# A decoder's quantised linear layer and long convolution, each as one streamed turn over eight batches

## The chip, the core and the metric

One core of a Trainium2 chip runs the whole program. The metric is the device time of one execution in microseconds (us); what is given for a kernel is the median of its runs.

## What is computed

The reference is a decoder of twelve sublayers over x of 8 batches x 256 rows x 256 columns, each followed by x = layernorm(x + sublayer(x)). The sixth and the seventh are at issue; the fifth, an attention with a side input over 16 heads, stands ahead of them.

```python
def quant_fp8(x):                                   # sixth: quantised linear layer
    amax = jnp.max(jnp.abs(x)).astype(jnp.float32)  # over the whole tensor
    scale = jnp.minimum(FP8_MAX / jnp.maximum(amax, 1e-12), FP8_MAX)   # FP8_MAX = 448
    return jnp.clip(x * scale, -FP8_MAX, FP8_MAX).astype(jnp.float8_e4m3fn), 1.0 / scale
w_fp8, w_scale = quant_fp8(weight)
x_fp8, x_scale = quant_fp8(x2d)
acc = jnp.matmul(x_fp8.astype(jnp.float32), w_fp8.astype(jnp.float32).T)
out2d = (acc * (x_scale * w_scale) + bias).astype(jnp.bfloat16)

p = (jnp.einsum('bld,de->ble', x, proj_w) + proj_b).reshape(B, L, order + 1, D)   # seventh: order = 2
v = p[:, :, 0, :]
for stage in range(order):
    vf = jnp.fft.rfft(v, n=fft_size, axis=1)
    ff = jnp.fft.rfft(filter_time[stage], n=fft_size, axis=1)
    v = jnp.fft.irfft(vf * ff, n=fft_size, axis=1)[:, :L, :] * p[:, :, stage + 1, :]
```

## The kernel before

Five engines run their own instruction lists: PE (matmuls and transposes into eight PSUM banks), DVE, ACT, POOL and SP (which issues the DMAs). Their only ties are semaphores. A `turn` (L215) is one block with a list for each engine, closed by a barrier of all engines. The order on each engine is the order in which the code issues. x stays in SBUF twice: `x_tok` with rows on partitions (16 tiles of 128x256) and `x_feat`, turned, with columns on partitions. All weights share one array, `weights`; `follow_weights` (L230) waits for a stage's weights and starts the load of the next stage's. Temporaries lie in `work`, and the profile calls them by that name.

The **side attention** (L2054) is one turn that streams 32 units (batch and four heads) through all engines; a step of its loop issues parts of several units, and `batch_statistics`, `batch_power`, `batch_normalise`, `batch_turn` and `batch_store` (L614 to L655) do the layernorm of one batch: statistics on DVE, the power -1/2 on POOL, the normalisation on DVE, four transposes on PE, the copy into `x_feat` on ACT.

The **quantised linear layer** (L2271) has a first turn: DVE takes the maximum of |x_tok| and of |w| on each partition (L2288, L2290), POOL takes them over the partitions (L2305), DVE works out the scales and rounds w to the values of e4m3 (L2259). A device loop then goes over four groups of two batches, a turn each: DVE rounds 1024 columns of x_feat in six operations (L2263 to L2268), PE multiplies (8 calls on bf16), DVE scales, adds bias and x (L2334, L2337), and the layernorm follows; its last copies are L420.

The **long convolution** (L2357) replaces the FFT by matmuls with 512x256 matrices `dft` and `idft`. A turn loads the weights, a turn makes the spectra of the two filters, then `run_late` (L364) issues the body for group 0, for groups 1 to 3 in a device loop, and a last turn with the tail alone. A body copies x (L272), projects it to three gates (24 calls of `mm`, L249; DVE adds the bias, L2442), and twice goes: four banks of forward transform (8 calls of 512 columns), eight products by the filter on DVE (L2453), four additions or subtractions on POOL (L2427), eight inverse calls (L2411), gate on DVE (L2459). The layernorm of the group before, the "late tail", stands between projection and transform. An fp32 matmul call shows as two MATMUL records in the profile.

## Time and profile before

| what | value |
|---|---|
| median of three runs | 2859.42 us (2854.62 to 2860.02) |
| the profiled execution, its own time | 2862.32 us |
| its span, first to last instruction | 2860.6 us |
| PE busy | 2333.3 us (82%), 12834 instructions |
| DVE busy | 1433.5 us (50%) |
| ACT busy | 1025.7 us (36%) |
| POOL busy | 672.5 us (24%) |
| mean granted clock of PE | 0.90 of 2.4 GHz |

The shares are means over twelve stages with different limits, so they don't say what binds one of them. A timeline row gives start, length, engine, line, operation, output and inputs, and in brackets how long the engine had idled and what released it. A granted clock of 1.00 is 2.4 GHz, 0.50 is 1.2 GHz; a stretch between the two had some of each.

### The profile page before, as it was taken

Reading aid. Unit: us, or ns where it says so; the run is one execution under the profiler, and the core shown is the slowest. Engines: PE = TensorE matmul, PEld = TensorE weight load, DVE = VectorE, ACT = ScalarE, POOL = GpSimd, SP = SyncE. Lnnn points to the kernel's source line nnn. Section 1 sums busy time; section 2 is a strip of 40 time slices with the busy share of each in tenths; the row PEclk is TensorE's granted clock in tenths of the full one; section 3 lists DMA queues with packets and bytes.
Section 4 is the critical chain, followed back from the end, with each engine's and each line's share of the span. In section 5 each row is a group of like instructions: output and inputs, shape, how many; then the busy total and the mean of one; then the engine's idle time right before and its main releaser. Section 6 shows DMA issues by size and latency. Waiting matters only on the chain. (4 is left out here: it accounts for less than half of the span.)

```text
span 2860.6 us, 38992 instructions
## 1 busy us (share of the span) xinstructions
PE 2333.3 (82%) x12834; PEld 1622.3 (57%) x12834; DVE 1433.5 (50%) x4235; ACT 1025.7 (36%) x2587; POOL 672.5 (24%) x609
## 2 busy tenths in 40 slices
PE   7983599878789438878667879879799899899898
PEld 5762477655467324447246656546356577466576
DVE  3554122447668554345412266645577543577454
ACT  3432111155446200006212226534366543466432
POOL 1113311200034102210443310065343200434111
PEclk9996799979789669988688989989899999999899
DMA  9041211290000100002157721130000000000000
GB/s 236 2 191 48 74 46 35 70 132 1 1 7 1 39 17 0 0 8 115 47 160 208 199 74 27 30 139 1 30 1 2 1 1 0 1 1 1 19 23 19
DMA packets 121167, 143.58 MB, mean 50 GB/s; under 512 B 47507, under 2 KB 101013, under 8 KB 119184
## 3 DMA queue, kind: packets, MB, share of 16 engines
q1 hardware_dynamic: 112240, 120.16, 15.7%
q0 software_dynamic: 8736, 20.99, 2.0%
q8 instruction: 105, 1.72, 0.3%
q14 instruction: 86, 0.70, 0.1%
HBM read 96.18 MB, written 47.90 MB: 50 GB/s over the span
## 5 line engine op out<-in xcount | busy, mean ns | idle before, releaser
L249 PE MATMUL bank<-work,weights 128*128 128x256 f32 (+4 forms) x2048 | 491.4, 397 | 65.0 <-DMA work<-in_weights 29.4
L249 PE MATMUL bank<-weights,work 128*128 128x256 f32 (+4 forms) x1680 | 450.8, 409 | 26.5 <-ACT work L272 16.9
L249 PEld LDWEIGHTS bank<-work,weights 128*128 128x128 f32 (+1 forms) x2048 | 345.7, 195 | 182.0 <-issue 50.7
L249 PEld LDWEIGHTS bank<-weights,work 128*128 128x128 f32 (+1 forms) x1680 | 314.5, 199 | 130.3 <-issue 59.0
L633 POOL TENSOR_TENSOR work<-work,minus_half 128x2 f32<-128x2 f32 x80 | 57.7, 722 | 801.2 <-DVE work L626 801.2
L249 PE MATMUL bank<-weights,x_feat 128*128 128x512 f32 (+2 forms) x384 | 166.2, 557 | 24.2 <-PEq L211 13.2
L249 PE MATMUL bank<-x_feat,weights 128*128 128x256 f32 (+3 forms) x400 | 119.3, 473 | 35.7 <-PEq L211 31.0
L249 PE MATMUL bank<-work 128*128 128x120 f32 (+4 forms) x358 | 82.2, 373 | 78.9 <-DVE work L2268 47.3
L3958 ACT ACTIVATE work<-work 128x128 f32<-128x128 f32 (+1 forms) x256 | 137.5, 545 | 1.7 <-DVE work L4030 1.6
L1523 DVE TENSOR_TENSOR work<-bank,work 128x384 f32<-128x384 f32 (+1 forms) x64 | 31.4, 491 | 190.0 <-ACT work L1441 190.0
L249 PEld LDWEIGHTS bank<-x_feat,weights 128*128 128x128 f32 (+1 forms) x400 | 79.6, 217 | 64.9 <-issue 51.5
L249 PEld LDWEIGHTS bank<-work 128*128 128x128 f32 (+2 forms) x358 | 59.6, 197 | 95.9 <-DVE work L2268 48.9
L249 PEld LDWEIGHTS bank<-weights,x_feat 128*128 128x128 f32 x384 | 68.7, 197 | 77.5 <-issue 59.1
L2898 ACT ACTIVATE work<-bank,work 128x128 f32<-128x128 f32 x124 | 38.9, 365 | 152.7 <-PE bank L249 144.0
L4350 DVE SCALAR_TENSOR_TENSOR work<-bank,weights,work 128x256 f32<-128x256 f32 x96 | 45.6, 482 | 86.6 <-ACT work L4288 85.5
L2756 POOL DMA_INDIRECT rows_back<-work x62 | 60.4, 974 | 115.4 <-DVE work L2994 97.0
L2994 DVE TENSOR_SCALAR work<-bank,work 128x256 f32<-128x256 f32 x62 | 30.0, 484 | 114.6 <-PE bank L249 98.6
L658 ACT COPY x_feat<-bank 128x512 f32<-128x512 f32 x64 | 37.4, 585 | 139.3 <-PE bank L650 138.9
L3773 POOL TENSOR_TENSOR work<-work,minus_half 128x8 f32<-128x8 f32 x32 | 52.4, 1638 | 142.3 <-DVE work L4074 142.3
L1341 POOL DMA_INDIRECT rows_back<-work x40 | 39.0, 974 | 195.4 <-DVE work L1531 195.4
L4288 ACT ACTIVATE work<-bank,weights 128x256 f32<-128x256 f32 x80 | 38.1, 476 | 127.9 <-PE bank L249 127.7
L4022 DVE CUSTOM_DVE_ANT_0 work<-bank,work 128x128 f32<-128x128 f32 (+1 forms) x256 | 75.9, 352 | 14.7 <-PE bank L3821 14.7
(462 smaller groups left out, 4750.2 us busy)
## 6 DMA issues: line engine op xcount, KB each, us to landing
weights<-in_weights SPq DMA_DIRECT2D x62, 256.0 KB
weights<-in_weights SPq DMA_DIRECT2D x1, 12296.0 KB, 35.5
weights<-in_weights SPq DMA_DIRECT2D x1, 9360.0 KB, 25.1
weights<-in_weights SPq DMA_DIRECT2D x1, 8488.0 KB, 23.9
work<-rows_in SPq DMA_DIRECT2D x62, 129.0 KB
rows_in<-ident SPq DMA_DIRECT2D x2, 3968.0 KB, 40.1
weights<-rows_back SPq DMA_DIRECT2D x8, 768.0 KB, 5.3
work<-rows_in SPq DMA_DIRECT2D x8, 645.0 KB, 4.2
```

Source lines behind the costliest of these rows:

```text
L249: ins = nc.tensor.matmul(out, lhsT, rhs, start=(i == 0), stop=(i == len(pairs) - 1))
L633: nc.gpsimd.tensor_tensor(t.rstd[:, n, :], t.rstd[:, n, :], K.minus_half[:, 0:2], ALU.pow).then_inc(K.S.rstd_done, 1)
L658: copy(K.x_feat[:, :, b * L:(b + 1) * L], K.bank[bank][:, :].rearrange("p (k t) -> p k t", k=KT)).then_inc(K.S.xT_stored, 1)
L1341: nc.gpsimd.indirect_dma_start(K.rows_back, bass.IndirectOffsetOnAxis(ap=to, axis=0), y[:, r, :], None, bounds_check=TOP * T - 1, oob_is_e ...
L1523: nc.vector.tensor_tensor(hT[:, q % 2, m, 0:n], K.bank[2 * (at % 2) + 1][:, 0:n], gelu[:, at % 2, 0:n], ALU.mult).then_inc(S.inner_stored, 1)
L2756: nc.gpsimd.indirect_dma_start(K.rows_back, bass.IndirectOffsetOnAxis(ap=to, axis=0), y[:, r, :], None, bounds_check=TOP * T - 1, oob_is_e ...
L2898: ins = nc.scalar.activation(hT[:, j % 2, m, :], K.bank[2 + j % 2][:, m * P:(m + 1) * P], ACT.Relu, bias=bias1[:, j % SETS, m:m + 1])
L3773: nc.gpsimd.tensor_tensor(rk, norm[:, 1, :], K.minus_half[:, 0:H], ALU.pow).then_inc(S.rk_done, 1)
L3958: ins = nc.scalar.activation(probs[:, u % 3, s, at:at + width], probs[:, u % 3, s, at:at + width], ACT.Exp, bias=bias[:, u % 2, i, s:s + 1 ...
L4022: ins = nc.vector.tensor_tensor_reduce(probs[:, u % 3, s, at:at + width], K.bank[SM[s]][:, at:at + width], seen[:, at:at + width], 1.0, -3 ...
L4288: nc.scalar.activation(gelu[:, n % 2, :], K.bank[n % RING][:, L:2 * L], ACT.Gelu, bias=W["b1"][:, layer, HT + f:HT + f + 1]).then_inc(S.ge ...
L4350: nc.vector.scalar_tensor_tensor(out=hid[rows, b % 2, f, :], in0=K.bank[n % RING][rows, 0:L], scalar=W["b1"][rows, layer, f:f + 1], in1=ge ...
```

## The change

Nothing changes in the arithmetic of a result but its grouping. Both stages become one turn each, unrolled over eight batches with double buffers, in the manner of the side attention.
- The maximum of |x_tok| is taken batch by batch inside the side attention, on DVE, one step after the batch is normalised, and that of |w| at its step 3. `quant_buffers` places the results and the rounded w behind the weights of the linear layer.
- In the linear layer, two transposes on PE with a reduction and a broadcast copy on DVE take the place of POOL's reduction over partitions. ACT multiplies x by its scale, DVE clamps it and makes the power of two (three operations of 512 columns), POOL adds and subtracts it.
- In the convolution a batch has its own 256-column calls: 12 of projection, 16 forward, 16 inverse, 4 transposes. The projection reads `x_feat` itself. The filter's spectra are stored with one part twice, so that two products of 512 columns replace four of 256; POOL's additions are 128x256. The load of the weights is waited for inside the turn, and that of the next stage's weights starts there.

Removed lines are in the functions printed above; the diff is cut to its core.

```diff
+def quant_buffers(K):
+    at = HIGH + words(5)
+    q = Names()
+    q.w16 = K.weights[:, at:at + KT * D // 2].bitcast(BF16).rearrange("p (k d) -> p k d", k=KT)
...
+    return q
 def side_attention(nc, K):
...
         @block.sync
...
+            def peak(b):
+                v.wait_ge(S.x_normed, b + 1)
+                nc.vector.tensor_reduce(q.peak[:, b:b + 1], K.x_tok[:, 2 * b:2 * b + 2, :].rearrange("p i d -> p (i d)"),
+                                        AX.X, ALU.max, apply_absolute_value=True)
...
                     c.finish(v, b)
+                if (b := at_step(t - BACK - 6, QUADS, B)) is not None:
...
                     store_v(b)
+                if t == 3:
+                    weights_are_in(v, K, 5)
+                    nc.vector.tensor_reduce(q.peaks[:, 1:2], next_w.rearrange("p k d -> p (k d)"), AX.X, ALU.max,
+                                            apply_absolute_value=True)
...
 def quantised_linear(nc, K):
...
+        def _(p):
+            def rounded(b):
+                p.wait_ge(S.k_rounded, b + 1)
+                nc.gpsimd.tensor_tensor(scaled[:, b % 2, :, :], scaled[:, b % 2, :, :], power[:, b % 2, :, :], ALU.add
+                                        ).then_inc(S.pool_step, 1)
+                p.wait_ge(S.pool_step, b + 1)
+                if b >= 2:
+                    p.wait_ge(S.y_done, b - 1)
+                nc.gpsimd.tensor_tensor(x16[:, b % 2, :, :], scaled[:, b % 2, :, :], power[:, b % 2, :, :], ALU.subtract
+                                        ).then_inc(S.xn_stored, 1)
...
+            def products(b):
+                pe.wait_ge(S.xn_stored, b + 1)
+                if b == 0:
...
+                if b >= 2:
+                    pe.wait_ge(S.bias_added, b - 1)
+                for i in range(2):
+                    ins = mm(nc, K.bank[b % 2][:, i * D:(i + 1) * D],
+                             [(x16[:, b % 2, k, i * P:(i + 1) * P], q.w16[:, k, :]) for k in range(KT)])
+                ins.then_inc(S.y_done, 1)
...
+            pe.wait_ge(S.max_done, 1)
+            nc.tensor.transpose(K.bank[4][0:2, 0:P], q.peaks, K.ident[:]).then_inc(S.aux_done, 1)
+            pe.wait_ge(S.spread_done, 1)
+            nc.tensor.transpose(K.bank[5][:, 0:2], spread_peaks[0:2, :], K.ident[0:2, 0:2]).then_inc(S.aux_done, 1)
...
+            def scale_x(b):
+                if b >= 2:
+                    a.wait_ge(S.xn_stored, b - 1)
+                nc.scalar.activation(scaled[:, b % 2, :, :], K.x_feat[:, :, b * L:(b + 1) * L], ACT.Copy, scale=q.scale[:, 0:1]
...
+            a.wait_ge(S.inverse_done, 1)
...
+            def magnitude(b):
+                v.wait_ge(S.xc_scaled, b + 1)
+                x = scaled[:, b % 2, :, :]
+                then(nc.vector.tensor_scalar(x, x, 448.0, -448.0, ALU.min, ALU.max))
+                then(nc.vector.tensor_scalar(power[:, b % 2, :, :].bitcast(I32), x.bitcast(I32), 0x7F800000, None,
+                                             ALU.bitwise_and))
+                nc.vector.tensor_scalar(power[:, b % 2, :, :], power[:, b % 2, :, :], 2.0 ** -6, 1.5 * 2.0 ** 20,
+                                        ALU.max, ALU.mult).then_inc(S.k_rounded, 1)
+            def residual(b):
+                x2 = K.x_tok[:, 2 * b:2 * b + 2, :]
+                v.wait_ge(S.y_done, b + 1)
+                nc.vector.scalar_tensor_tensor(
+                    out=y16[:, b % 2, :, :], in0=K.bank[b % 2][:, :].rearrange("p (i d) -> p i d", i=2),
+                    scalar=q.out_scale, in1=W["bias"].broadcast_to([P, 2, D]), op0=ALU.mult, op1=ALU.add
+                    ).then_inc(S.bias_added, 1)
+                v.wait_ge(S.bias_added, b + 1)
+                nc.vector.tensor_tensor(x2, x2, y16[:, b % 2, :, :], ALU.add).then_inc(S.residual_done, 1)
+                batch_statistics(nc, v, K, tail, b)
+            nc.vector.tensor_reduce(q.peaks[:, 0:1], q.peak, AX.X, ALU.max).then_inc(S.max_done, 1)
             v.wait_ge(S.aux_done, 1)
...
+            then(nc.vector.tensor_reduce(q.most[0:2, :], K.bank[4][0:2, 0:P], AX.X, ALU.max))
+            nc.vector.tensor_copy(spread_peaks[0:2, :], q.most[0:2, :].broadcast_to([2, P])).then_inc(S.spread_done, 1)
+            v.wait_ge(S.aux_done, 2)
+            then(nc.vector.tensor_scalar(q.scale, K.bank[5][:, 0:2], 1e-12, None, ALU.max))
+            then(nc.vector.reciprocal(q.scale, q.scale))
+            nc.vector.tensor_scalar(q.scale, q.scale, 448.0, 448.0, ALU.mult, ALU.min).then_inc(S.inverse_done, 1)
+            v.wait_ge(S.inverse_done, 1)
+            then(nc.vector.reciprocal(q.back, q.scale))
+            then(nc.vector.tensor_tensor(q.out_scale, q.back[:, 0:1], q.back[:, 1:2], ALU.mult))
+            for t in range(STEPS):
+                if (b := at_step(t, 1, B)) is not None:
+                    magnitude(b)
+                if t == 0:
+                    round_to_e4m3(nc, then, q.w16, W["w"], q.scale[:, 1:2], w_scaled, w_power).then_inc(S.root_done, 1)
+                if (b := at_step(t - 1, 1, B)) is not None:
+                    residual(b)
+                if (b := at_step(t - 2, 1, B)) is not None:
+                    batch_normalise(nc, v, K, tail, b)
...
 def long_convolution(nc, K):
...
+    ORDER, STEPS = 2, B + 4
+    GATES, HALVES, BACK, X = (0, 1, 2), (3, 4), (5, 6), 7
+    gates = A(2, ORDER + 1, 2 * D)
+    filt = A(ORDER, 2, 3 * D)
+    part = A(2, 2, 2 * D)
+    spec = A(2, 4, D)
...
+            def combine(q):
+                for f in range(2):
+                    p.wait_ge(S.probs_done, 2 * q + f + 1)
+                    if q >= 2:
+                        p.wait_ge(S.out_done, q - 1)
+                    for which, op in ((0, ALU.subtract), (1, ALU.add)):
+                        ins = nc.gpsimd.tensor_tensor(spec[:, q % 2, f + 2 * which, :], part[:, f, which, 0:D],
+                                                      part[:, f, which, D:2 * D], op)
+                    ins.then_inc(S.pool_step, 1)
...
+            def project(b, e):
+                if b:
+                    pe.wait_ge(S.q_stored, 3 * (b - 1) + e + 1)
+                for i in range(2):
+                    ins = mm(nc, K.bank[GATES[e]][:, i * D:(i + 1) * D],
+                             [(K.x_feat[:, k, b * L + i * P:b * L + (i + 1) * P], W["proj"][:, k, e * D:(e + 1) * D])
+                              for k in range(KT)])
+                ins.then_inc(S.qk_done, 1)
...
+            def forward(b, s):
+                q = 2 * b + s
+                if s:
+                    pe.wait_ge(S.gate_done, b + 1)
+                else:
+                    pe.wait_ge(S.q_stored, 3 * b + 1)
+                for f in range(2):
+                    if q:
+                        pe.wait_ge(S.probs_done, 2 * (q - 1) + f + 1)
+                    else:
+                        pe.wait_ge(S.aux_stored, 1)
+                    for m in (f, f + 2):
+                        ins = mm(nc, K.bank[HALVES[f]][:, m // 2 * D:(m // 2 + 1) * D],
+                                 [(W["dft"][:, k, m * P:(m + 1) * P], gates[:, b % 2, 0, k * D:(k + 1) * D])
+                                  for k in range(2)])
+                    ins.then_inc(S.scores_done, 1)
+            def backward(b, s):
+                q = 2 * b + s
+                pe.wait_ge(S.pool_step, 2 * q + 2)
+                if b == 0:
+                    pe.wait_ge(S.aux_stored, 2)
+                else:
+                    pe.wait_ge((S.gate_done, S.y_added)[s], b)
+                for m in range(2):
+                    ins = mm(nc, K.bank[BACK[s]][:, m * D:(m + 1) * D],
+                             [(W["idft"][:, n, m * P:(m + 1) * P], spec[:, q % 2, n, :]) for n in range(4)])
+                ins.then_inc(S.out_done, 1)
...
+            for t in range(STEPS):
+                if (b := at_step(t, 1, B)) is not None:
+                    forward(b, 0)
+                if (b := at_step(t + 1, 1, B)) is not None and b:
+                    project(b, 0)
+                    project(b, 1)
+                if (b := at_step(t - 1, 1, B)) is not None:
+                    backward(b, 1)
+                if (b := at_step(t, 1, B)) is not None:
+                    backward(b, 0)
+                if (b := at_step(t + 1, 1, B)) is not None and b:
+                    project(b, 2)
+                if (b := at_step(t - 2, 1, B)) is not None:
+                    turn_x(b)
+                if (b := at_step(t, 1, B)) is not None:
+                    forward(b, 1)
...
+                a.wait_ge(S.aux_done, s + 1)
...
+                    nc.scalar.copy(filt[:, s, f, 0:2 * D], bank[:, :])
+                    ins = nc.scalar.copy(filt[:, s, f, 2 * D:3 * D], bank[:, 0:D])
+                ins.then_inc(S.aux_stored, 1)
...
+            def store_gates(b, e):
+                v.wait_ge(S.qk_done, 3 * b + e + 1)
+                if b >= 2:
+                    v.wait_ge((S.scores_done, S.gate_done, S.residual_done)[e], (4 * b - 4, b - 1, b - 1)[e])
+                nc.vector.tensor_tensor(gates[:, b % 2, e, :].rearrange("p (i d) -> p i d", i=2),
+                                        K.bank[GATES[e]][:, :].rearrange("p (i d) -> p i d", i=2),
+                                        W["bproj"][:, :, e * D:(e + 1) * D].broadcast_to([P, 2, D]), ALU.add
+                                        ).then_inc(S.q_stored, 1)
+            def filtered(b, s):
+                q = 2 * b + s
+                if q < 2:
+                    v.wait_ge(S.aux_stored, q + 1)
+                for f in range(2):
+                    v.wait_ge(S.scores_done, 2 * q + f + 1)
+                    if q:
+                        v.wait_ge(S.pool_step, 2 * (q - 1) + f + 1)
+                    for which in range(2):
+                        ins = nc.vector.tensor_tensor(part[:, f, which, :], K.bank[HALVES[f]][:, :],
+                                                      filt[:, s, f, which * D:(which + 2) * D], ALU.mult)
+                    ins.then_inc(S.probs_done, 1)
+            def gate(b):
+                v.wait_ge(S.out_done, 2 * b + 1)
+                v.wait_ge(S.q_stored, 3 * b + 2)
+                nc.vector.tensor_tensor(gates[:, b % 2, 0, :], K.bank[BACK[0]][:, :], gates[:, b % 2, 1, :], ALU.mult
+                                        ).then_inc(S.gate_done, 1)
+            def residual(b):
+                x2, y = K.x_tok[:, 2 * b:2 * b + 2, :], gates[:, b % 2, 2, :]
+                v.wait_ge(S.out_done, 2 * b + 2)
+                v.wait_ge(S.q_stored, 3 * b + 3)
+                nc.vector.tensor_tensor(y, K.bank[BACK[1]][:, :], y, ALU.mult).then_inc(S.y_added, 1)
...
+            for t in range(STEPS):
+                if (b := at_step(t, 1, B)) is not None:
+                    filtered(b, 0)
+                if (b := at_step(t + 1, 1, B)) is not None and b:
+                    store_gates(b, 0)
+                    store_gates(b, 1)
+                if (b := at_step(t - 1, 1, B)) is not None:
+                    residual(b)
+                if (b := at_step(t, 1, B)) is not None:
+                    gate(b)
+                if (b := at_step(t - 1, 1, B)) is not None:
+                    batch_normalise(nc, v, K, tail, b)
+                if (b := at_step(t + 1, 1, B)) is not None and b:
+                    store_gates(b, 2)
+                if (b := at_step(t, 1, B)) is not None:
+                    filtered(b, 1)
```

PE in the long convolution, before: a pass of the loop over groups, from the late tail's transposes to the end of the first of two filter stages (`bankN` is a PSUM bank, 128x512 the output of a call).

```order
L413 MATMUL bank6<-ident,work 128x128 x4
L413 MATMUL bank7<-ident,work 128x128 x4
L249 MATMUL bank0<-work,weights 128x512 x2
L249 MATMUL bank2<-work,weights 128x512 x2
L249 MATMUL bank1<-work,weights 128x512 x2
L249 MATMUL bank3<-work,weights 128x512 x2
L2411 MATMUL bank4<-work,weights 128x512 x2
L2411 MATMUL bank5<-work,weights 128x512 x2
```

The same engine now, one step of the stream: forward transform of batch b (banks 3, 4), projection of b+1 (0, 1, 2), inverse of b-1 (6) and of b (5), transposes of b-2 (7), second forward transform of b.

```order
L249 MATMUL bank3<-work,weights 128x256 x4
L249 MATMUL bank4<-work,weights 128x256 x4
L249 MATMUL bank0<-weights,x_feat 128x256 x4
L249 MATMUL bank1<-weights,x_feat 128x256 x4
L249 MATMUL bank6<-work,weights 128x256 x8
L249 MATMUL bank5<-work,weights 128x256 x8
L249 MATMUL bank2<-weights,x_feat 128x256 x4
L650 MATMUL bank7<-ident,x_tok 128x128 x4
L249 MATMUL bank3<-work,weights 128x256 x4
L249 MATMUL bank4<-work,weights 128x256 x4
```

Between a forward transform and its inverse there stood nothing of another batch before; now there stand the projection of the next batch and an inverse of the one before.

DVE in the linear layer now, one step: clamp and power of batch b, residual and statistics of b-1, normalisation of b-2.

```order
L2377 TENSOR_SCALAR work<-work 128x512
L2378 TENSOR_SCALAR work<-work 128x512
L2380 TENSOR_SCALAR work<-work 128x512
L2386 SCALAR_TENSOR_TENSOR work<-bank,weights 128x512
L2391 TENSOR_TENSOR x_tok<-x_tok,work 128x512
L619 BN_STATS work<-x_tok 128x6 x2
L623 BN_AGGR work<-work 128x2 x2
L626 TENSOR_SCALAR work<-work 128x2
L641 TENSOR_SCALAR x_tok<-x_tok,work 128x256 x2
```

Before, all of this was one chain per group of two batches, with the multiplication by the scale and both roundings on DVE too.

## Rows read from the trace of the kernel before

**Rows 1.** Busy time by stretch, with granted clock (PEclk)
```profile
core 0: us, PE busy (x) PEld busy (x) DVE busy (x) ACT busy (x) POOL busy (x), PEclk, DMA share, GB/s
826.00:945.00 119.00, 116.14 (x913) 82.66 (x911) 102.95 (x203) 72.67 (x126) 51.98 (x33) 1.00 0.01 1
...
983.00:1051.00 68.00, 16.02 (x64) 9.89 (x64) 49.16 (x100) 6.90 (x12) 5.98 (x8) 0.50 0.00 0
...
1065.40:1111.50 46.10, 39.13 (x112) 20.71 (x112) 18.58 (x29) 0.62 (x1) 9.99 (x8) 1.00 0.00 0
1111.50:1167.20 55.70, 44.43 (x120) 23.80 (x120) 22.23 (x44) 2.35 (x4) 11.47 (x10) 0.90 0.00 1
```

**Rows 2.** Timeline (start, length, what, idle before), PE, convolution
```profile
1054.18 8.71 PE L249 MATMUL bank<-weights 128*128 128x256 f32 x32 [3.99 <-PEq L211]
1066.13 10.63 PE L249 MATMUL bank<-weights,work 128*128 128x256 f32 x48 [3.24 <-ACT work L272]
1077.55 7.13 PE L249 MATMUL bank<-work,weights 128*128 128x512 f32 x16 [0.78 <-DVE work L2442]
...
1112.40 12.08 PE L249 MATMUL bank<-weights,work 128*128 128x256 f32 x48 [4.35 <-ACT work L272]
...
1129.84 10.10 PE L249 MATMUL bank<-work,weights 128*128 128x512 f32 x16 [4.49 <-DVE work L2442]
```

**Rows 3.** Timeline, DVE, end of side attention to end of convolution
```profile
961.33 0.69 DVE L747 TENSOR_TENSOR x_tok<-x_tok,bank 128x512 f32<-128x512 f32 x1 [6.61 <-PE bank L249]
...
963.12 0.17 DVE L626 TENSOR_SCALAR work<-work 128x2 f32<-128x2 f32 x1
964.10 0.73 DVE L641 TENSOR_SCALAR x_tok<-x_tok,work 128x256 f32<-128x256 f32 x2 [0.81 <-POOL work L633]
967.98 4.42 DVE L2288 TENSOR_REDUCE work<-x_tok 128x1 f32<-128x4096 f32 x1 [3.14 <-PEq L211]
972.31 0.68 DVE L2290 TENSOR_REDUCE work<-weights 128x1 f32<-128x512 f32 x1
977.07 0.17 DVE L2295 TENSOR_SCALAR work<-work 128x2 f32<-128x2 f32 x1 [4.09 <-POOL work L2305]
...
978.47 0.43 DVE L2264 TENSOR_SCALAR work<-work 128x512 f32<-128x512 f32 x1
...
980.58 0.69 DVE L2268 TENSOR_TENSOR work<-work 128x512 bf16<-128x512 f32 x1
...
989.75 0.75 DVE L2334 SCALAR_TENSOR_TENSOR work<-bank,work,weights 128x512 bf16<-128x512 f32 x1 [1.13 <-PE bank L249]
990.66 0.69 DVE L2337 TENSOR_TENSOR work<-work,x_tok 128x512 f32<-128x512 bf16 x1 [0.16 <-DVE work L2334]
...
1050.34 0.69 DVE L420 COPY x_feat<-bank 128x512 f32 x1 [1.32 <-PE bank L413]
...
1282.83 0.69 DVE L420 COPY x_feat<-bank 128x512 f32<-128x512 f32 x1 [1.21 <-PE bank L413]
```

**Rows 4.** Timeline, PE and ACT: half clock, stage ends
```profile
965.80 0.59 ACT L658 COPY x_feat<-bank 128x512 f32<-128x512 f32 x1 [8.34 <-PE bank L650]
...
988.68 1.89 PE L249 MATMUL bank<-work 128*128 128x256 bf16 x8 [22.92 <-DVE work L2268]
995.85 2.12 PE L413 MATMUL bank<-ident,work 128*128 128x128 f32 x8 [5.28 <-DVE work L327]
...
1284.82 1.94 PE L2505 MATMUL bank<-ident,weights 128*128 128x128 f32 x8 [2.03 <-PEq L211]
```

**Rows 5.** Timeline, side attention: DVE beside POOL, and DVE's wait
```profile
886.58 1.79 POOL L2077 TENSOR_TENSOR work<-work 128x960 f32<-128x960 f32 x1 [1.64 <-DVE work L2237]
...
886.85 1.99 DVE L641 TENSOR_SCALAR x_tok<-x_tok,work 128x256 f32<-128x256 f32 x2
...
896.75 1.22 DVE L2230 TENSOR_TENSOR work<-bank,weights 128x480 f32<-128x480 f32 x2 [2.07 <-PE bank L2118]
```

**Rows 6.** Timeline, long convolution: DVE and POOL side by side
```profile
1081.28 2.49 DVE L2453 TENSOR_TENSOR work<-bank,work 128x512 f32<-128x512 f32 x4 [3.79 <-PE bank L249]
...
1082.65 2.50 POOL L2427 TENSOR_TENSOR work<-work 128x512 f32<-128x512 f32 x2 [34.41 <-DVE work L2453]
```

222 lines of the change are left out of this document (77 added, 145 removed).

## The prediction

> **What bounds the kernel now.** The program is a row of stages with a barrier between them, so I read stage by stage. First the table of stretches [rows 1]. The side attention fills PE: 116.14 of 119 us at clock 1.00. The quantised linear layer fills nothing: PE works 16.02 of 68.00 us, DVE 49.16. Of the long convolution's four group bodies the first takes 46.10 us with PE busy 39.13, the second 55.70 with PE 44.43 and DVE 22.23; the other two are like it. Then the timelines of one group. PE's work at full clock is a projection (10.63 us), four blocks of 7.13 us and, from the second group on, eight transposes [rows 2]. Between them PE waits for DVE and POOL, and in the later groups it starts at half clock: the projection takes 12.08, the first transform 10.10. So the convolution is a chain of waits around about 40 us of PE work per group, and its bound should be PE. The linear layer is a chain on DVE [rows 3]: one reduction of all x_tok (4.42 us), 4.09 us idle for POOL's reduction over partitions, then four groups in 68 us, with DVE idle at each hand-over (1.13 us ahead of L2334).
>
> **Linear layer.** Before, it runs from DVE's first instruction at 967.98 to the end of the last copy, 1050.34 + 0.69 = 1051.03: 83.05 us [rows 3]. After, I build it up in the order of its DVE rows.
> - Start. A reduction of 128x8, a transpose, a reduction of 2x128, a copy, a transpose and three small operations take the place of 9.1 us (967.98 to 977.07). Small DVE operations are 0.17 long and about 0.20 apart, six of them 1.2; two transposes at half clock, 0.27 each by 2.12 / 8 [rows 4], with hand-overs of about 0.2 each, 1.0. ACT scales from 970.2. Its 0.6 and the three operations of the clamp and the power (0.43 each, 0.46 apart, 1.35 together) end at 972.3. The Trainium skill (GPSIMD Engine Reference, Engine selection) wants a reduction over partitions on GpSimd; the 4.09 us of idle speak for PE in this case, and by that rule the start would keep about 3 us more.
> - Rounding of w, on DVE beside POOL's rounding of batch 0: four operations at 0.46 and two at 0.72, 3.3 us, plus about 2.5 if two POOL operations of 1.27 hold it up. Ends at 978.1.
> - A steady step on DVE: clamp and power 1.35, scalar_tensor_tensor to the end of the residual 1.60 (989.75 to 991.35), statistics 1.25 (the end of the residual at 962.02 to 963.29), normalise 0.73, 0.12 of waits: 5.05 us. POOL's load is 2 x 1.27 + 0.70 = 3.2, PE's 1.89 / 2 + 1.06 = 2.0, ACT's 1.2. DVE sets the pace. POOL's result for batch b comes some 4.5 us after the clamp of b ends and is read 5 us after it, so this wait is just covered.
> - Contention. In the side attention a normalise of 2 x 256 columns takes 1.99 us where POOL has just begun a 1.79 us operation, against 0.73 without one [rows 5]: it stood still for 1.26. Here POOL runs two large operations per batch beside DVE. Bounds: 0 and 2 x 1.26 per step; I take 0.65, since much of what DVE does then reads PSUM, as L2453 does, which runs at its 0.62 a piece beside POOL [rows 6]. The Trainium skill (SBUF — State Buffer, section SBUF: two separate sides) calls this an exclusive lock of a port pair, taken by DVE's two-port modes and also by DVE operations with two SBUF inputs; with that the residual's add would be held up too, about 0.7 a step, so 5.75 instead of the 5.05 without contention. The row of 1.99 agrees for the normalise; no row here shows the case of two SBUF inputs.
> - So 978.1, first clamp and residual 4.9, six steps of 5.7, then residual 7 and normalise 6 (4.1), and power wait, normalise 7, transposes at half clock and store (2.5): 1023.8. The layer takes 55.8 us: **27.2 us less**. Bounds 22 and 34 (steps of 6.4 and 5.05).
>
> **Long convolution.** Before: 1051.03 to 1283.52 (1282.83 + 0.69 [rows 3]), 232.5 us. After, with PE never waiting in the steady steps:
> - PE's work does not change. The 512-column calls become twice as many of 256 columns, and 16 MATMUL records of 512 cost 7.13 us, 48 of 256 cost 10.63 [rows 2]: 0.446 and 0.221 each, the same per column. Eight transposes take 1.06, half of their 2.12 at half clock [rows 4]. Per two batches 10.63 + 4 x 7.13 + 1.06 = 40.2; four times, 160.8. The filters' 32 records at 0.221 are 7.1.
> - Cold clock once. The filters cost 8.71 instead of 7.1, the second group 4.4 us more than the first [rows 2]. Bounds 1.6 and 4.4, I take 3.0. Each of three later groups pays 4.4 now, and this goes.
> - The start, 1.3 (1283.52 to 1284.82, where the next stage's PE begins [rows 4]). The load's own turn, the filters' turn and the last tail's turn go, with their barriers: the weights are issued a layer earlier in both kernels and are there.
> - Waits at the end. The last forward transform must pass DVE (two of 0.62 after 0.16) and POOL (two of 128x256) before the inverse. POOL's 128x256 is in no row; 128x512 is 1.27 [rows 6], so 0.64 to 1.27 each: 2.8 to 4.0, I take 3.2. The gate of batch 7 has a transpose less and no projection behind it: 0.4.
> - Tail after the last product: 5.06 as in the side attention (961.33 to 966.39 [rows 3, 4]) plus 0.16 and 0.86 for the multiplication ahead of it, less 0.5 of transposes already counted: 5.6.
> Sum 160.8 + 7.1 + 3.0 + 1.3 + 3.2 + 0.4 + 5.6 = 181.4: **51.1 us less**.
>
> Does PE really not wait? Take the order of the step. The first inverse of batch b comes 7.1 us after its spectrum (8 calls of projection, 8 of inverse, 0.44 a call). DVE and POOL need 0.16 + 1.3 + 0.07 + 1.3 to 2.5: under 4.1. A half of the transform is 1.77 us, DVE takes it away in 1.5, and the bank is wanted again 1.77 after its end: slack 0.25, the thinnest place. The gate needs 0.9 behind the inverse, the projection and the transposes cover 2.3; DVE must have finished the residual of b-1 by then (2.9 of 3.5). DVE's load per batch is 3 x 0.62 + 8 x 0.62 + 0.7 + 2.9 + 0.7 = 11.2 of 20.1 us, POOL's 8 x 0.64 to 1.27 plus 0.7: 5.8 to 10.9.
>
> **Side attention.** Eight reductions of 128x512 (0.68 each, as L2290 [rows 3]) and one of w. That of w stands where DVE idles at the stage's start. DVE idles 2.07 us behind the place of the others in each batch, and PE has no wait there [rows 5]: 0, at most 6 x 0.68 = 4.1 if it passes on.
>
> **Sum.** 27.2 + 51.1 = 78.3. The profiled execution took 2862.3 with a span of 2860.6; the median is 2859.4, 3 us lower, and I subtract from the median: **2781 us**. The terms' bounds: 22 to 34, 40 to 54 (a stall of 1.4 us per batch; the cold start at its least), 0 to -4: 2771 to 2801.
>
> **Rivals.**
> 1. PE bound fails at the thin place: DVE or POOL comes late for a bank and PE waits some 2 us in each batch. For it: slack of 0.25 us; POOL's 128x256 without a row. Against it: DVE is 56% loaded. Gives 2781 + 16 = 2797.
> 2. The linear layer's contention is near total: POOL's 3.2 us a batch stand beside none of DVE's work, step 5.05 + 3.2 = 8.25. Gives 2781 + 8 x 2.55 = 2801. For it: the row of 1.99. Against it: POOL and DVE overlap freely in the convolution's rows.
> 3. Slower: with PE filled without a pause, the granted clock falls to 1.2 GHz for the whole stage. The 168 us of PE work would double and the time be 2781 + 165 = 2946. It decides from about half of the work at half clock (78 of 168). Against it: 119 us of the side attention with PE busy for 116.14 ran at 1.00, while half clock (0.50) shows in the linear layer, where PE stands idle most of the time [rows 1].
> 4. The change doesn't do what it says: the turns are streamed but a wait chains each batch to the next (residual of b before forward of b+1, say). By the order of the instructions no such wait stands there; it would give back most of the 51 us, some 2825.
>
> **Chances.** Forecast 0.70, rival 1 0.14, rival 2 0.09, rival 4 0.04, rival 3 0.03. I widen the range to 2766 to 2804 for rivals 1 and 2. Within 0.2% (6 us) a measurement of this kernel can hardly tell a difference from none. All but rival 3 are faster by more: faster 0.96, same 0.01, slower 0.03.
>
> **What would show it.** In the profile after: the convolution about 181 us long with PE busy over 95% in its middle at clock 1.0, a step of 20.1 us per batch, and no wait of PE on DVE or POOL over 0.3 us before the last batch; the linear layer about 56 us long with DVE packed, steps of 5.1 to 6.4; the side attention still 154 us. A step over 21 us in the convolution, or a clock under 0.95 there, makes the forecast wrong; so does a linear layer over 62 us.

## The result, and the profile after

The changed kernel takes 2774.51 us (median of 4 runs, 2773.58 to 2779.8), the kernel before 2858.53 (4 runs, 2854.62 to 2860.02): a ratio of 0.9712, 95% interval 0.9695 to 0.9729, 84 us less. Forecast were 2781 and 78 less.

I measure each layer as the prediction did, from its first DVE instruction to the end of its last copy:

```
layer              before   forecast   after    difference
side attention     172.8    172.8      172.8      0.0
linear layer        83.05    55.8       64.0    -19.1
long convolution   232.5    181.4      176.0    -56.5
to expert layer's first load, in all           -76.4
expert layer, 62 loads of weights
                   161.6    161.6      153.5     -8.1
```

(Side attention: from PE's first product after the previous barrier, 795.20 and 796.36, to DVE's next layer, 967.98 and 969.12. The forecast said "still 154 us" of a shorter stretch, 812.0 to 966.4; it put the change there at nothing, and that is what the table's forecast stands for.) The row "in all" also holds what lies between and behind the layers, 0.8 us less. The expert layer is code that the change doesn't touch; it is taken up below.

Stretches of the changed kernel, in the columns of [rows 1]: the linear layer whole, the steady part of the convolution, the convolution whole.

```profile
969.00:1033.00 64.00, 16.44 (x66) 9.45 (x66) 45.46 (x110) 9.74 (x16) 29.11 (x24) 0.50 0.11 44
1060.00:1187.00 127.00, 127.00 (x600) 111.26 (x599) 72.54 (x135) 2.93 (x5) 43.72 (x62) 1.00 0.00 1
1034.37:1208.96 174.59, 166.87 (x768) 144.91 (x768) 89.02 (x168) 7.83 (x16) 50.75 (x72) 0.98 0.02 7
```

The second line shows where the convolution's gain comes from: PE is busy 127.00 of 127.00 us at clock 1.00, where the second group of before had 44.43 of 55.70 at 0.90. The first line shows a layer that still fills nothing: DVE 45.46 of 64.

Timeline of PE in the convolution, the counterpart of [rows 2]: one whole step, and the end.

```profile
1157.20 7.07 PE L249 MATMUL bank<-work,weights 128*128 128x256 f32 x32
1164.11 3.62 PE L249 MATMUL bank<-weights,x_feat 128*128 128x256 f32 x16
1167.56 7.07 PE L249 MATMUL bank<-work,weights 128*128 128x256 f32 x32
1174.47 1.89 PE L249 MATMUL bank<-weights,x_feat 128*128 128x256 f32 x8
1176.20 0.60 PE L650 MATMUL bank<-ident,x_tok 128*128 128x128 f32 x4
1176.63 13.98 PE L249 MATMUL bank<-work,weights 128*128 128x256 f32 x64
1190.45 0.60 PE L650 MATMUL bank<-ident,x_tok 128*128 128x128 f32 x4
1191.39 3.72 PE L249 MATMUL bank<-work,weights 128*128 128x256 f32 x16 [0.35 <-DVE work L2571]
1197.98 5.41 PE L249 MATMUL bank<-work,weights 128*128 128x256 f32 x16 [2.86 <-POOL work L2447]
```

From 1157.20 to 1176.63 is one step, 19.43 us, with no wait in it; the two waits at the end are the ones forecast as 0.4 and 3.2. The rows' lengths overlap: each shows about 0.16 us of pipeline behind the start of the next, so 32 calls take 6.91 us (1157.20 to 1164.11), 0.216 each.

All engines in one step of the linear layer, the counterpart of the DVE rows at 989.75 in [rows 3]:

```profile
998.39 0.43 DVE L2377 TENSOR_SCALAR work<-work 128x512 f32<-128x512 f32 x1 [2.45 <-ACT work L2360]
...
999.82 1.26 POOL L2313 TENSOR_TENSOR work<-work 128x512 f32<-128x512 f32 x1 [3.64 <-DVE work L2380]
1000.43 1.20 DVE L2391 TENSOR_TENSOR x_tok<-x_tok,work 128x512 f32<-128x512 f32 x1
1001.16 1.59 POOL L2318 TENSOR_TENSOR work<-work 128x512 bf16<-128x512 f32 x1
...
1002.81 1.03 PE L249 MATMUL bank<-weights,work 128*128 128x256 bf16 x4 [5.70 <-POOL work L2318]
1002.81 0.73 DVE L641 TENSOR_SCALAR x_tok<-x_tok,work 128x256 f32<-128x256 f32 x2
...
1003.69 1.09 PE L650 MATMUL bank<-ident,x_tok 128*128 128x128 f32 x4
1004.82 0.58 ACT L658 COPY x_feat<-bank 128x512 f32<-128x512 f32 x1 [6.46 <-PE bank L650]
1005.30 0.72 ACT L2360 ACTIVATE work<-x_feat,weights 128x512 f32<-128x512 f32 x1
1006.05 0.43 DVE L2377 TENSOR_SCALAR work<-work 128x512 f32<-128x512 f32 x1 [2.51 <-ACT work L2360]
```

The step is 7.66 us, not 5.7, and DVE idles 2.5 of it. It waits for ACT to scale the next batch; ACT's scaling stands behind the store of an older batch, which waits for that batch's transposes on PE. That is a circle through all the queues, and the experiments ask which instructions are in it.

### The profile page after: what moved, and what is told of

It reads as the page before. It is cut to its first block and busy times, and to the rows that moved or that the text cites. A ratio compares the mean times of both kernels' runs of the same rounds, so it can differ in the third digit from the quotient of the medians.

```text
span 2773.1 us, 39253 instructions
## 1 busy us (share of the span) xinstructions
PE 2315.0 (83%) x13092; PEld 1663.2 (60%) x13092; DVE 1422.1 (51%) x4229; ACT 1025.0 (37%) x2591; POOL 699.1 (25%) x656
## 5 line engine op out<-in xcount | busy, mean ns | idle before, releaser
L249 PE MATMUL bank<-work,weights 128*128 128x256 f32 (+3 forms) x2432 | 541.3, 380 | 42.2 <-DMA work<-in_weights 21.1
L249 PEld LDWEIGHTS bank<-work,weights 128*128 128x128 f32 (+1 forms) x2432 | 415.5, 193 | 138.2 <-DMA work<-in_weights 27.8
L249 PE MATMUL bank<-weights,work 128*128 128x256 f32 (+4 forms) x1520 | 412.6, 409 | 53.1 <-POOL work L2318 35.0
L249 PEld LDWEIGHTS bank<-weights,work 128*128 128x128 f32 (+1 forms) x1520 | 278.5, 196 | 152.7 <-issue 68.3
L633 POOL TENSOR_TENSOR work<-work,minus_half 128x2 f32<-128x2 f32 x96 | 69.7, 726 | 859.0 <-DVE work L626 859.0
L249 PE MATMUL bank<-weights,x_feat 128*128 128x512 f32 (+2 forms) x576 | 211.5, 500 | 25.5 <-PEq L211 14.6
L658 ACT COPY x_feat<-bank 128x512 f32<-128x512 f32 x80 | 46.7, 584 | 343.3 <-PE bank L650 342.9
L249 PEld LDWEIGHTS bank<-weights,x_feat 128*128 128x128 f32 x576 | 106.1, 196 | 84.2 <-issue 60.1
L650 PE MATMUL bank<-ident,x_tok 128*128 128x128 f32 x320 | 61.2, 325 | 46.1 <-DVE x_tok L641 44.0
L249 PE MATMUL bank<-work 128*128 128x256 f32 (+3 forms) x326 | 72.9, 362 | 31.1 <-ACT work L2692 7.6
```

The costliest lines, as they stand in the source:

```text
L249: ins = nc.tensor.matmul(out, lhsT, rhs, start=(i == 0), stop=(i == len(pairs) - 1))
L633: nc.gpsimd.tensor_tensor(t.rstd[:, n, :], t.rstd[:, n, :], K.minus_half[:, 0:2], ALU.pow).then_inc(K.S.rstd_done, 1)
L650: ins = nc.tensor.transpose(K.bank[bank][:, (2 * k + i) * P:(2 * k + i + 1) * P], K.x_tok[:, 2 * b + i, k * P:(k + 1) * P], K.ident[:])
L658: copy(K.x_feat[:, :, b * L:(b + 1) * L], K.bank[bank][:, :].rearrange("p (k t) -> p k t", k=KT)).then_inc(K.S.xT_stored, 1)
```

## Experiments

Each kernel was timed beside the kernel before on the same chip. "Layer" is measured as above.

**1. The convolution's stream alone.** The linear layer and the side attention are the functions of before.

> The changed kernel with the linear layer and the side attention of before; only the convolution is streamed. By the stretches of the changed kernel's trace the convolution gives 56.5 us (232.5 to 176.0) and the linear layer 19. Theory A (the two gains stand beside each other and add up): 2858.5 - 56.5 = 2802. Rival (a good part of the gain is in the shared parts, such as the clock left over from one stage to the next, or in the stages behind): the two single gains don't add up to 84; this one would be under 50 or over 65. The expert layer behind, whose code is not changed, took some 9 us less in the profile after; if that is scatter, it takes anything between 154 and 162 us here.

Measured: 2800.0 us (2794.61 to 2805.03), ratio 0.9809 [0.9792, 0.9827], 55 us below before and 2 below what was expected.

**2. The linear layer alone.** `long_convolution` is the function of before.

> The changed kernel with the convolution of before; the maxima in the side attention and the linear layer are the changed ones. Theory A: the linear layer goes from 83.1 to 64.0 us, so 2858.5 - 19 = 2839.5. Rival: the maxima in the side attention cost some us that the linear layer gives, then its stretch is longer than 154 us and the gain under 15.

Measured: 2830.97 (2829.53 to 2843.22), ratio 0.9912 [0.9898, 0.9926], 24.5 below before. Its linear layer takes 63.98 us, to 0.01 that of the changed kernel. That is 8.5 us below the 2839.5 expected from the layer's 19.1. The seven executions fall into two groups, five at 2829.5 to 2831.0 and two at 2842.1 and 2843.2, and the traced one is of the second; why one kernel takes two times 12 us apart stays open. The parts add up: 55 + 24.5 = 80 against 84. So neither leans on the other, the convolution brings about two thirds, and the linear layer is short of its forecast by itself.

**3. ACT stores a step later.** The scaling of b+1 no longer stands behind the store of b-2.

```diff
-    STEPS = B + 3
+    STEPS = B + 4
...
-                if (b := at_step(t - 2, 1, B)) is not None:
+                if (b := at_step(t - 3, 1, B)) is not None:
                     batch_store(nc.scalar.copy, a, K, b, 2 + b % 2)
```

> The changed kernel, where ACT stores the turned x of a batch one step later in the linear layer, so that the scaling of the next batch is queued ahead of it. Theory A (the step of 7.6 us is a circle through the queues: scaling, clamp on DVE, two operations on POOL, product and transposes on PE, store on ACT, next scaling): the circle opens and the step falls to what DVE and POOL need, 5.5 to 6; six steps, 10 to 12 us off, some 2763. Rival B (DVE and POOL stop each other at their SBUF port and that is what the step is made of): no change, 2774, step still 7.6.

Measured: 2762.79 (2757.56 to 2767.42), ratio 0.9672 [0.9657, 0.9688], below the changed kernel's interval. The step on all engines:

```profile
999.00 0.42 DVE L2377 TENSOR_SCALAR work<-work 128x512 f32<-128x512 f32 x1
...
1000.35 0.59 ACT L658 COPY x_feat<-bank 128x512 f32<-128x512 f32 x1 [3.86 <-PE bank L650]
...
1000.83 0.72 ACT L2360 ACTIVATE work<-x_feat,weights 128x512 f32<-128x512 f32 x1
1001.03 1.20 DVE L2391 TENSOR_TENSOR x_tok<-x_tok,work 128x512 f32<-128x512 f32 x1
...
1004.06 0.42 DVE L2377 TENSOR_SCALAR work<-work 128x512 f32<-128x512 f32 x1
```

The step falls from 7.66 to 5.06, and DVE has no idle time ahead of L2377: ACT's work for the next batch is done 2.5 us before DVE wants it. The layer takes 51.1 us in place of 64.0. One position in one queue cost 12.8 us. The step is below the 5.5 to 6 that was expected; rival B, no change, is out.

**4 to 6. Which arc closes the circle?** Two instructions could hold the store: the transposes of b-2 stand behind the products of b on PE (these wait for POOL's rounding), and they need the normalise of b-2, the last work of DVE's step. Experiment 4 swaps the first, 5 the second, 6 both.

```diff
+                if (b := at_step(t - 2, 1, B)) is not None:
+                    turn_x(b)
                 if (b := at_step(t, 1, B)) is not None:
                     products(b)
-                if (b := at_step(t - 2, 1, B)) is not None:
-                    turn_x(b)
...
+                if (b := at_step(t - 2, 1, B)) is not None:
+                    batch_normalise(nc, v, K, tail, b)
                 if (b := at_step(t - 1, 1, B)) is not None:
                     residual(b)
-                if (b := at_step(t - 2, 1, B)) is not None:
-                    batch_normalise(nc, v, K, tail, b)
```

> The changed kernel, where PE turns batch b-2 ahead of the product of batch b instead of behind it. Theory A: the same circle is cut at another place, since the transposes no longer wait for POOL; the step falls to 5.5 to 6 and the time to some 2763. Rival B: no change. If this one helps and the later store doesn't, the circle isn't the one I describe.

> The changed kernel with one swap on DVE in the linear layer: in each step the normalise of batch b-2 stands ahead of the residual of batch b-1. PE's order is the changed kernel's: products of b, then transposes of b-2. Theory A (one arc): the only arc that sets the 7.6 us step goes over DVE's normalise (scaling of b+1 on ACT, store of b-2, transposes of b-2, normalise at the end of DVE's step). Then the step falls to about 5.1 us and the kernel gains some 12 us: about 2763. Theory B (two arcs of nearly the same length): the transposes of b-2 also stand behind the products of b on PE, and these wait for POOL's rounding of b; in the changed kernel the product ended at 1003.84 and the normalise at 1003.54. Then the step stays at 7.3 to 7.7 us and the time within 2 us of the changed kernel: about 2774.

> The changed kernel with both swaps in the linear layer: normalise of b-2 ahead of the residual of b-1 on DVE, and transposes of b-2 ahead of the products of b on PE; ACT's order stays. Theory B (two arcs): only together do they shorten the circle: clamp and power 1.4, normalise 0.7 and its hand-over, four transposes 1.1, store 0.6, scaling 0.7, with hand-overs 4.9 to 5.2 us, about DVE's own 5.07. Step 5.1 to 5.4 us, the kernel 11 to 13 us below the changed one: about 2763. Theory A (one arc over the normalise): the same time as norm_first. If ACT's queue isn't what holds the step, no gain: 2774.

```
                   median (range)                ratio [interval]         step   layer
changed kernel     2774.51                       0.9712 [.9695, .9729]    7.66   64.0
PE swapped (4)     2775.56 (2774.71-2783.19)     0.9724 [.9709, .9739]    7.66   65.8
DVE swapped (5)    2773.38 (2770.42-2775.51)     0.9709 [.9696, .9722]    7.36   64.4
both (6)           2769.04 (2760.87-2776.88)     0.9700 [.9685, .9715]    5.86   57.0
```

Experiment 4 refuted what I had first put down as the only route, over POOL and the products. Its trace shows the other arc:

```profile
1000.78 0.73 DVE L641 TENSOR_SCALAR x_tok<-x_tok,work 128x256 f32<-128x256 f32 x2
...
1001.66 1.09 PE L650 MATMUL bank<-ident,x_tok 128*128 128x128 f32 x4 [5.72 <-DVE x_tok L641]
...
1002.78 0.58 ACT L658 COPY x_feat<-bank 128x512 f32<-128x512 f32 x1 [6.45 <-PE bank L650]
1003.26 0.72 ACT L2360 ACTIVATE work<-x_feat,weights 128x512 f32<-128x512 f32 x1
1004.02 0.43 DVE L2377 TENSOR_SCALAR work<-work 128x512 f32<-128x512 f32 x1 [2.51 <-ACT work L2360]
```

Each swap alone leaves the step at 7.4 to 7.7; only both bring it down. (The layer of experiment 4 is 1.8 us longer at the same step, because the last product now stands behind a batch's transposes: its reader on DVE starts 7.28 us after the last step's start, against 5.49 in the changed kernel.) So two arcs of nearly the same length close on the same store, as the changed kernel's own rows say (the product ended at 1003.84, the normalise at 1003.54). The step of 5.86 in the last, not 5.1 to 5.4, has its reason mainly in one row: the normalise now stands beside POOL's first addition.

```profile
1003.56 0.43 DVE L2380 TENSOR_SCALAR work<-work 128x512 f32<-128x512 f32 x1
1003.90 1.68 DVE L641 TENSOR_SCALAR x_tok<-x_tok,work 128x256 f32<-128x256 f32 x2
1004.07 1.36 POOL L2313 TENSOR_TENSOR work<-work 128x512 f32<-128x512 f32 x1 [0.44 <-DVE work L2380]
```

1.68 in place of 0.73, while the residual's add takes 1.05 in place of 1.20: together 0.80, which is what 5.86 has over the 5.06 of experiment 3. DVE has no idle time in this step either. In the layer this version gains 7.0 us; by median only 5.5, and its interval meets the changed kernel's. That it is faster rests on the layer's rows.

**7. The rounding of x on DVE.** On top of experiment 3, POOL's two additions become two DVE operations behind the power.

> The version store_later with the two additions of the rounding of x on DVE in place of POOL. My theory: DVE is that version's bound (step 5.07 us). It gains two operations of 0.72 a step and loses what POOL's operations hold up, 0.5 on the residual's add and up to 1.9 once on the rounding of w: step 5.9 to 6.1 us, 7 x 0.9 - 1.9 = about 4 us slower than store_later, 2767. The row of the residual's add (128x512, two SBUF inputs) reads 0.69 again in place of 1.20, if POOL beside it was what doubled it. Rival: POOL's hold on DVE costs as much as it takes off, and the time is that of store_later within 1 us or below it.

Measured: 2770.86 (2766.47 to 2773.51), ratio 0.9697 [0.9684, 0.9711], 8 us above experiment 3 where about 4 were expected; layer 56.9, 5.8 more, step 6.01 as expected. The residual's add, with nothing on POOL beside it, first here, then that of the last batch in the changed kernel itself, when POOL has no more additions:

```profile
999.58 0.69 DVE L2384 TENSOR_TENSOR x_tok<-x_tok,work 128x512 f32<-128x512 f32 x1
```

```profile
1027.65 0.69 DVE L2391 TENSOR_TENSOR x_tok<-x_tok,work 128x512 f32<-128x512 f32 x1
```

0.69, as L2337 in [rows 3], in place of 1.20. So POOL's additions held it up by 0.51, and POOL still takes off more (two operations, 1.44 us a step) than it costs.

**8. The maxima over partitions on GpSimd.**

```diff
-            nc.tensor.transpose(K.bank[4][0:2, 0:P], q.peaks, K.ident[:]).then_inc(S.aux_done, 1)
...
-            then(nc.vector.tensor_reduce(q.most[0:2, :], K.bank[4][0:2, 0:P], AX.X, ALU.max))
...
+            nc.gpsimd.partition_all_reduce(all_peaks, q.peaks, P, bass.bass_isa.ReduceOp.max).then_inc(S.aux_done, 1)
```

> The changed kernel with the maxima over partitions taken by one GpSimd reduction over partitions, as before, in place of two transposes on PE, a reduction of 2x128 and a copy on DVE. My theory: the start's gain from PE is the 4.05 us from the end of DVE's maxima to the end of GpSimd's reduction in the kernel before, against 1.35 us over PE and DVE (969.28 to 970.63): the first scaling on ACT starts about 2.7 us later and the kernel is 2.7 us slower than the changed one, about 2777. Rival (GpSimd's first use of that operation had cost loading that the earlier 4 us hid, or the rounding of w covers the start): 0 or over 5 us.

Measured: 2789.65 (2788.79 to 2793.71), ratio 0.9771 [0.9757, 0.9784]: 15 us slower than the changed kernel, not 2.7. Timeline, POOL and DVE:

```profile
964.90 0.69 POOL L633 TENSOR_TENSOR work<-work,minus_half 128x2 f32<-128x2 f32 x1 [9.87 <-DVE work L626]
...
969.42 0.16 DVE L2392 TENSOR_REDUCE weights<-weights 128x1 f32<-128x8 f32 x1 [2.34 <-PEq L211]
978.77 0.37 POOL L2322 PARTITION_ALL_REDUCE work<-weights  x1 [13.19 <-issue]
979.18 0.17 DVE L2394 TENSOR_SCALAR weights<-work 128x2 f32<-128x2 f32 x1 [9.59 <-POOL work L2322]
...
986.29 1.28 POOL L2313 TENSOR_TENSOR work<-work 128x512 f32<-128x512 f32 x1 [7.14 <-issue]
```

and the same instruction in the kernel before:

```profile
963.37 0.69 POOL L633 TENSOR_TENSOR work<-work,minus_half 128x2 f32<-128x2 f32 x1 [9.87 <-DVE work L626]
...
976.67 0.37 POOL L2305 PARTITION_ALL_REDUCE work<-work  x1 [12.61 <-issue]
```

From the operand to the result it took 4.05 us before and 9.56 here. From the end of POOL's previous instruction it took 12.98 and 13.55 (and 13.06 in experiment 1, which has the old linear layer): nearly the same. So it did from the layer's first DVE instruction, 9.06 and 9.72 (8.91 in experiment 1); these runs don't tell which of the two it starts from, and what POOL does in that time no row shows. The operation stands once in each program, so a price of its first use isn't told apart from one of every use. Either way the 4.09 us of idle DVE in [rows 3] was not this operation's price but what stood out of it behind DVE's two maxima, 5.0 us (967.98 to 972.99). Behind it POOL idles another 7.14 us for no operand ("issue"), though the first batch's power was ready at 981.97. That was hidden before, where POOL had nothing to do until 994.10. The layer takes 73.7 us, 9.7 more; the expert layer's loads, whose code is the same, take 5.5 more in this trace, about the rest of the median's 15.

**9. The convolution without cover.** On PE each inverse transform directly follows its own forward transform.

```diff
+                if (b := at_step(t - 1, 1, B)) is not None:
+                    backward(b, 1)
                 if (b := at_step(t, 1, B)) is not None:
                     forward(b, 0)
+                    backward(b, 0)
                 if (b := at_step(t + 1, 1, B)) is not None and b:
                     project(b, 0)
                     project(b, 1)
-                if (b := at_step(t - 1, 1, B)) is not None:
-                    backward(b, 1)
-                if (b := at_step(t, 1, B)) is not None:
-                    backward(b, 0)
```

> The changed kernel with PE's order in the convolution altered: each inverse transform stands right behind its own forward transform (inverse of b-1 for the second order at the start of the step, forward and inverse of b for the first order, then the projections), with no projection or other inverse between. My theory: what hides DVE's multiplication and POOL's combination is the other batch's PE work between; without it PE waits for POOL as at the end of the changed kernel, 2.86 us, twice in each batch, less what the last batch waits already: 14 x 2.86, about +40 us, range +30 to +50: about 2814. The step goes from 19.4 to about 25 us. Rival (the gain of the convolution is the clock and the fewer group starts, not the cover): under +10 us.

Measured: 2857.69 (2851.96 to 2867.19), ratio 1.0004 [0.9993, 1.0014]: 83 us slower than the changed kernel, where about 40 were expected, and as much as the whole gain of the change. PE's rows of one batch, then three stretches of 28 to 30 us (columns: us, PE busy, clock):

```profile
1120.14 3.72 PE L249 MATMUL bank<-work,weights 128*128 128x256 f32 x16 [1.82 <-DVE work L2570]
1126.72 8.86 PE L249 MATMUL bank<-work,weights 128*128 128x256 f32 x32 [2.86 <-POOL work L2447]
1138.44 5.34 PE L249 MATMUL bank<-work,weights 128*128 128x256 f32 x16 [2.86 <-POOL work L2447]
```

```profile
1081.20:1108.98 27.78, 19.80 (x89) 1.00 0.00 1
1108.98:1137.00 28.02, 21.92 (x92) 0.94 0.00 1
1138.40:1168.00 29.60, 23.53 (x92) 0.89 0.00 0
```

Three waits, 7.54 us a batch, and not the two I had counted: the gate is no longer covered either. (DVE's order was left as it was, with the gate of b behind the gates of b+1, whose projections PE now issues later; so this third wait comes of the two orders not fitting each other as well as of the missing cover.) And the clock falls, from 1.00 in the first of the stretches to 0.94 and 0.89: 32 calls that cost 7.07 take 8.86, 16 take 5.34 in place of 3.72. A batch comes to 28 to 32.5 us instead of 19.43; the layer to 254.9, longer than the 232.5 of before. So one turn and one batch at a time gain nothing by themselves; the chain of waits is now gone through eight times, where the kernel before had four groups of two batches. That this makes the difference is an explanation that no run here tests.

**10. Half of the cover.** Only the two projections move, behind both inverses.

> The changed kernel with the two projections of batch b+1 moved on PE from between forward and inverse to behind both inverses: the forward of b, the second-order inverse of b-1 and the first-order inverse of b now follow each other, so that 16 calls of 256 columns (3.5 us), not 32 or 48, stand between a forward transform and its inverse. DVE's order is unchanged. Theory: the way over DVE and POOL needs 2.86 us, 3.5 us of cover are enough, and no wait of PE on POOL appears in the middle. But DVE takes the residual of b-1 and the gate of b behind the gates of b+1, which now come late: PE waits for the gate of b, 1.82 us in each of 7 batches as cover_gone showed with the same rows. So about 13 us more than the changed kernel, 2787, if the granted clock stays 1.00; if that one pause in a batch lowers the clock as the three pauses of cover_gone did (0.89 to 0.94 in its steps of 28 to 31 us), up to 10 us more: 2797.

Measured: 2793.99 (2788.2 to 2797.45), ratio 0.9785 [0.9772, 0.9799], 19 us above the changed kernel; layer 194.7, 18.7 more.

```profile
1049.78 5.41 PE L249 MATMUL bank<-work,weights 128*128 128x256 f32 x16 [2.86 <-POOL work L2447]
...
1104.86 14.08 PE L249 MATMUL bank<-work,weights 128*128 128x256 f32 x64 [1.82 <-DVE work L2571]
1118.78 5.34 PE L249 MATMUL bank<-weights,x_feat 128*128 128x256 f32 x24
1123.95 0.60 PE L650 MATMUL bank<-ident,x_tok 128*128 128x128 f32 x4
1126.37 14.08 PE L249 MATMUL bank<-work,weights 128*128 128x256 f32 x64 [1.82 <-DVE work L2571]
```

```profile
1080.00:1100.00 20.00, 18.34 (x77) 0.91 0.00 0
1100.00:1120.00 20.00, 18.18 (x87) 1.00 0.00 1
```

POOL's wait is gone wherever 3.5 us of cover stand. It is there, 2.86 us at 1049.78, for the one inverse that has none: that of batch 0, with no batch before it and its neighbour's projections moved behind it. The gate's wait is there as read from experiment 9, 2.25 once and 1.82 five times (batch 7 has 0.34, as in the changed kernel). A batch takes 21.51 us, 2.08 more: the wait of 1.82 and 0.26 around it. Six such batches make 12.9 of the 18.7, batch 0's wait 3.1. The other 2.6 are the clock: 1.7 in the stretch at 0.91, right behind the wait of 2.25 (64 calls in 15.77, not 14.08), and 0.9 at the layer's start. A further 1.7 at 1049.78 (16 calls in 5.41, not 3.72) cancel out, since the changed kernel pays them at its end and this one doesn't. So these pauses cost their own length and a little more, and the three of experiment 9 some 3 us a batch more by the clock (31.07 us at 1126.72, against 27.78 at 1098.94).

## Why the prediction was right, and where it was off

The side, the range and the cause held: 2774.5 lies in 2766 to 2804. But the two layers gave 75.6 us where 78.3 were forecast, and the parts were off in opposite directions by more than the sum: 5.4 too long and 8.2 too short. Both layers even lie outside the bounds I gave them: 56.5 against 40 to 54 for the convolution, 19.1 against 22 to 34 for the linear layer (and by my own steps of 6.4 and 5.05 those would have been about 23 and 31). That the sum of the two came within 3 us of the measured one is luck. Another 8 us, which no part of the change explains, took the median to 84 below; without them it would be about 2783, in the range as well.

- **Convolution: right in kind, 5.4 us too long.** "PE never waiting in the steady steps" is what the rows show: the stretch of 127.00 us, waits of 0.35 and 2.86 at the end (forecast 0.4 and 3.2), start 1.3 (1.27). The mis-sized term is PE's work, 160.8: I divided a row's length by its calls (10.63 by 48), and such a row holds about 0.2 us of pipeline that lies beside the next. From start to start a call costs 0.216 and a batch 19.43, against 20.1: eight times 0.67 is the 5.4. The cold clock, put at 3.0 and once, shows in two places, 1.9 at the start (24 calls in 7.08 us, not 5.18) and 1.7 behind the wait of 2.86 at the end (16 in 5.41, not 3.72). POOL's 128x256, bounded by 0.64 and 1.27, takes 0.70 (two in 1.41), the near end, as the thin place needed.
- **Linear layer: 8.2 us too short**, and over the 62 us that I had named as the mark of a wrong forecast. The start was right (ACT scales 2.1 us after DVE's first instruction, forecast 2.2), so was the hold-up of w's rounding in kind (two operations at 1.37 against 0.43, 1.9 us of the 2.5). The step that failed is "DVE sets the pace": I added up each engine's load and followed POOL's result to its reader, but did not follow ACT's queue, where the scaling of b+1 waits behind a store. Experiment 3 shows what the step is without it: 5.06, on the 5.05 that I had for a DVE without contention, and not 5.7. The contention was there (0.51 on the residual's add), but DVE's neighbouring instructions overlap by about as much, which my sum didn't credit.
- **Rule and row.** The Trainium skill (SBUF — State Buffer, section SBUF: two separate sides) names DVE operations with two SBUF inputs among those that lock the port pair. By that the residual's add had to be held up, and it is: 1.20 beside POOL, 0.69 alone (experiment 7), 0.51 where I had worked out about 0.7. The Trainium skill (GPSIMD Engine Reference, Engine selection) would give the reduction over partitions to GpSimd; I put this at 3 us more, and the run shows 9.7 in the layer.
- **Side attention at nothing: right, as far as two traces can say.** 172.8 us in both. Behind the reductions (0.67 to 0.69 each) DVE's wait falls from 2.07 to 1.47, and that of batch 7 at 966.04 lies beside the last transposes. But this stage scatters by 7 us between traces of the same code (below).
- **Rival 4** (a wait chains the batches) is what happened, but in the linear layer and over one position in ACT's queue, where I had looked for it in the convolution. Rivals 1 and 3 did not happen; rival 2's time for the linear layer's step, 8.25, was near the measured 7.66, for another reason.
- **The other 8 us.** In the traces of the twelve kernels, with this layer's code the same, the expert layer's 62 loads of weights span 153.5 to 163.1 us: 153.5 in the changed kernel, 154.4 to 156.4 in five of the others, 159.0 to 162.0 in four, 161.6 in the one before, 163.1 in that of experiment 2. The side attention's code differs in no experiment with the changed linear layer, and spans 165.6 to 172.8. No edit orders these numbers, and executions of one kernel scatter as much: fifteen of the kernel before lie between 2852.6 and 2862.1, the seven of experiment 2 between 2829.5 and 2843.2. So I count the 8 us as scatter, whose cause stays open, and not as the change's; that is argued from these numbers, and no run isolates it. It hides the forecast's miss in the linear layer, and makes medians 5 us apart weak evidence here: I go by the layer's own rows.

The fastest version found is experiment 3, 2762.79 us: 12 us below the changed kernel and 96 below the one before.

## What to carry to other kernels

When batches are streamed through in-order queues, add up each engine's load, then walk each wait through the queue of the engine that serves it, as far as the instruction that it feeds: a copy in front of the next batch's first operation closes a circle that no load shows. Where a swap gains nothing, look for a second arc of the same length before the theory is dropped. And let the bound engine keep another batch's work between a producer and its consumer; what is lost without it is the waits and, once they add up, the clock.

## What the runs showed that I had not expected

- GpSimd's reduction over partitions ended 13.0 to 13.6 us after POOL's previous instruction and 8.9 to 9.7 after the layer's first DVE instruction, in three traces, though its operand was ready 3.9 us before its result in one and 9.6 in another. Where POOL's next instruction was wanted at once, it started 7.1 us behind it (one trace). Beside other work this is invisible; on the path it was 9.7 us.
- The clock fell only where PE paused, but not at each pause: 1.00 with none, and with one of 1.8 us in each 21.5 but for the stretch behind the first, of 2.25 us (0.91); with three in each batch, 7.5 to 8 us in all, 0.89 to 0.94, but 1.00 in one batch that had 8.0 us of them (1081.20 to 1108.98). So the lost cover cost 79 us in the layer, where the waits alone make 53 (7 times 7.54); most of the rest is the clock.
- The hold-up between DVE and POOL works both ways: where DVE's add takes 1.20, POOL's second addition takes 1.59, and 1.26 at the shortest elsewhere.
